# Router logits from the second norm's transposes: centred gate weights, context taken through the gates, choices for four tiles at a time

## What is computed

```
x = x + tanh(g_xattn[0]) * cross_attention_32_heads(layernorm(x), ctx)
x = x + tanh(g_ffn[0])   * (layernorm(x) @ W.T + bias)          # W dequantised
x = x + tanh(g_xattn[1]) * softmax(Q K.T * scale) @ ctx         # Q from layernorm(x), K from ctx
x = x + tanh(g_ffn[1])   * mixture_of_experts(layernorm(x))     # 32 experts, top 2
```

## Time and profile before

| what | us |
|---|---|
| median of 3 runs (883.96 to 884.87) | 884.09 |
| profiled execution | 882.28 |
| its span | 880.5 |
| first section (32 heads) ends | about 622 |
| first transposes of the second section (line 1803) | 622.53 |
| `score(0)` starts | 668.25 |
| `turn(0)` starts, the expert slots follow | 728.65 |
| TensorE's granted clock, mean over the span | 0.975 |

### The profile page before, as it was taken

One profiled execution on the slowest core, in us unless ns is written; L12 is line 12 of the kernel. 1 busy time (PEld: TensorE's weight loads), 2 busy tenths in 40 slices (PEclk: granted clock), 3 DMA queues, 4 the chain that ended last, 5 costly groups with the idle time before them and its releaser, 6 DMA issues. The chain is left out here.

```text
span 880.5 us, 13114 instructions
## 1 busy us (share of the span) xinstructions
PE 825.1 (94%) x4337; PEld 695.1 (79%) x4337; DVE 653.5 (74%) x1285; ACT 397.2 (45%) x1010; POOL 438.0 (50%) x386
## 2 busy tenths in 40 slices
PE   5889999999999999999999999999999999999980
PEld 4678888888888888888888888788778687778860
DVE  3888888867778876778876777856691658999965
ACT  4645245234334424324433433443314537879960
POOL 5489648436437634634833643530200148888840
PEclk9999999999999999999999999999999959999995
DMA  8401101101201100110220210100620677989517
GB/s 329 177 1 49 72 1 63 58 1 48 73 1 48 71 0 0 62 58 1 76 91 0 95 48 1 49 1 1 235 82 1 263 269 249 340 313 362 220 42 287
DMA packets 25945, 91.13 MB, mean 104 GB/s; under 512 B 6576, under 2 KB 7088, under 8 KB 18848
## 3 DMA queue, kind: packets, MB, share of 16 engines
q1 hardware_dynamic: 19744, 81.00, 25.1%
q0 software_dynamic: 6144, 9.46, 3.0%
HBM read 86.23 MB, written 14.68 MB: 115 GB/s over the span
## 5 line engine op out<-in xcount | busy, mean ns | idle before, releaser
L402 POOL TENSOR_TENSOR qT<-straight,turned 128x512 f32<-128x512 f32 x64 | 83.1, 1300 | 141.8 <-DVE turned L652 141.5
L518 ACT ACTIVATE probs<-bank,negmax 128x128 f32<-128x128 f32 x256 | 90.4, 365 | 130.8 <-DVE negmax L663 130.8
L652 DVE TENSOR_TENSOR turned<-bank,sinT 64x512 f32<-64x512 f32 x160 | 110.1, 688 | 2.2
L129 PE MATMUL bank<-xT_hi,wq_hi 128*128 128x512 f32 x256 | 104.2, 407 | 2.0 <-DVE xT_lo L105 2.0
L525 ACT ACTIVATE pT_hi<-bank 128x512 fp32r<-128x512 f32 x64 | 38.2, 598 | 139.0 <-PE bank L823 139.0
L131 PE MATMUL bank<-xT_hi,wq_lo 128*128 128x512 f32 x256 | 100.2, 392 | 0.0
L130 PE MATMUL bank<-xT_lo,wq_hi 128*128 128x512 f32 x256 | 100.0, 391 | 0.0
L131 PE MATMUL bank<-wo_hi,oT_lo 128*128 128x512 f32 x256 | 99.8, 390 | 0.0
L129 PE MATMUL bank<-wo_hi,oT_hi 128*128 128x512 f32 x256 | 99.7, 389 | 0.0
L130 PE MATMUL bank<-wo_lo,oT_hi 128*128 128x512 f32 x256 | 99.6, 389 | 0.0
L650 DVE TENSOR_TENSOR straight<-bank,cosT 128x512 f32<-128x512 f32 x80 | 55.3, 691 | 40.7 <-PE bank L131 36.9
(11 more groups left out here) (232 smaller groups left out, 2082.5 us busy)
## 6 DMA issues: line engine op xcount, KB each, us to landing
ring<-in_ew SPq DMA_DIRECT2D x28, 1024.0 KB, 8.8
raw_big<-in_wq SPq DMA_DIRECT2D x8, 1024.0 KB, 4.8
raw_big<-in_wo SPq DMA_DIRECT2D x8, 1024.0 KB, 4.8
early_w<-in_ew SPq DMA_DIRECT2D x8, 1024.0 KB, 10.0
ring<-picked SPq DMA_DIRECT2D x8, 512.0 KB, 7.6
raw_k<-in_wk SPq DMA_DIRECT2D x8, 256.0 KB, 5.1
ctx_raw<-in_ctxT SPq DMA_DIRECT2D x4, 512.0 KB, 6.1
raw_v<-in_wv SPq DMA_DIRECT2D x8, 256.0 KB, 5.0
```

The costliest lines, as they stand in the source:

```text
L129: nc.tensor.matmul(out_, hi, r_hi, start=start, stop=False)
L402: nc.gpsimd.tensor_tensor(dst, straight[:, k, :], turned[:, k, :], ALU.add).then_inc(rope_sum, 1)
L518: ex = nc.scalar.activation(probs[:, u % 2, h, :], bank_scores[u % 2][:, h * S:(h + 1) * S], ACT.Exp, bias=negmax[:, u % UNITS, h:h + 1], ...
L652: last = nc.vector.tensor_tensor(turned[dst, k, :], bank[src, :], sinT[src, tok], ALU.mult)
```

## The change

The last norm is linear in x up to a mean and a scale for each token, so a logit can be had without the normed row. The mean falls away if the gate weights are centred (from each column its mean is taken off). What is left is the centred gate on x, which is the second norm's turned tile times its own spread plus the attended part. The kernel after therefore makes, ahead of the router:

- on POOL, ACT and PE, the centred gate weights as an upper and a lower part side by side (`gate_pair`), with the mean from a matmul with a constant matrix;
- on PE, `wide(0..3)`: `gate_pair` times the context (0, 1) and times the turned second norm (2, 3), in 8 matmuls each; ACT keeps them (`wide_keep`), PE turns and joins the two parts (`wide_turn`);
- `ctx_gates` (ACT) and `base` (DVE) of these. The logits of four tiles are then one matmul each of the attention weights with `ctx_gates` (`gate_scores`), scaled and added to `base`.

`choose`, `code`, `find_place`, `rank` and the marks work on four tiles (marks on two) in place of one. The router's transposes, their copies on ACT and the old logits are gone. The order of SP's expert weights is changed, and ring slot 11 is no longer loaded at the section's start, since the new small tensors lie there. The diff, cut to its core:

```diff
@block.sync
-                for k in (*range(EARLY), RING):
+                for k in range(EARLY):
                     sp.dma_start(ring[k], a["ew"][k]).then_inc(w_in[k], 16)
...
+                sp.wait_ge(g_mm, 4 * KC)
+                first_weights(3, 4)
                 sp.wait_ge(g_smm, 2)
-                for k in (*range(EARLY, RING - 4), RING - 2, RING - 1):
-                    sp.dma_start(ring[k], a["ew"][k]).then_inc(w_in[k], 16)
-                keep_rows(TILES)
+                first_weights(2)
+                keep_rows(range(0, 4))
+                first_weights(5)
+                keep_rows(range(4, 6))
+                first_weights(6)
+                keep_rows(range(6, 8))
                 sp.wait_ge(g_omm, NB)
-                for k in range(RING - 4, RING - 2):
-                    sp.dma_start(ring[k], a["ew"][k]).then_inc(w_in[k], 16)
+                first_weights(7, 8, 9, 10)
+                sp.wait_ge(r_logits, 2)
+                first_weights(11)
@block.gpsimd
+                nc.gpsimd.memset(mean_of[:, :], 1.0 / E).then_inc(gate_step, 1)
+                pool.wait_ge(g_tables, 64)
+                pool.wait_ge(gate_step, 3)
+                nc.gpsimd.tensor_tensor(centred[:, :, :], gw[:, :, :], gate_mean[:, :].unsqueeze(1).broadcast_to([P, KC, NX]), ALU.subtract).then_inc(gate_step, 1)
+                pool.wait_ge(gate_step, 5)
+                nc.gpsimd.tensor_tensor(gate_pair[:, :, NX:], centred[:, :, :], gate_pair[:, :, 0:NX].bitcast(F32), ALU.subtract).then_inc(gate_step, 1)
                 weights_rest(1)
...
@block.scalar
                 for c in range(KC):
                     act.wait_ge(f_turned, c + 1)
                     nc.scalar.activation(wT_hi[:, c, :], psum[4 + c][:, :], ACT.Copy).then_inc(f_hi, 1)
+                act.wait_ge(gate_step, 2)
+                nc.scalar.activation(gate_mean[:, :], psum[2][:, 0:NX], ACT.Copy).then_inc(gate_step, 1)
                 norm_upper(act, 1, 4)
...
-                router_norm(0)
-                router_norm(1)
-                router_kept(0)
+                for t in range(0, 4):
+                    router_norm(t)
...
@block.vector
+                def choose(h):
+                    tiles = range(4 * h, 4 * h + 4)
+                    dve.wait_ge(gate_step, 8)
+                    dve.wait_ge(r_logits, h + 1)
+                    for b, t in enumerate(tiles):
+                        nc.vector.scalar_tensor_tensor(base[:, t, :], psum[1][:, t * NX:(t + 1) * NX], l1scale[:, b:b + 1], base[:, t, :],
+                                                       ALU.mult, ALU.add).then_inc(r_best, 1)
...
                 softmax_shift(0)
                 softmax_scale(0)
+                scale_base()
                 dve.wait_ge(g_tables, 64)
+                choose(0)
                 attended(0)
                 attended(1)
                 softmax_shift(1)
+                find_place(0)
                 attended(2)
                 attended(3)
                 softmax_scale(1)
+                mark_places(0)
+                mark_places(1)
+                choose(1)
+                normed(0)
                 attended(4)
-                normed(0)
                 attended(5)
+                find_place(1)
+                normed(1)
+                mark_places(2)
                 attended(6)
...
+                mark_places(3)
                 attended(7)
...
                 normed(2)
...
@block.tensor
+                def wide(n):
...
+                    for c in range(KC):
+                        if c:
+                            nc.tensor.matmul(bank[0:NX, :], gate_pair[:, c - 1, 0:NX], r_lo[:, c - 1, half_of(n % 2)], start=False, stop=False)
...
+                        mm = nc.tensor.matmul(bank[0:2 * NX, :], gate_pair[:, c, :], r_hi[:, c, half_of(n % 2)], start=c == 0, stop=c == KC - 1)
+                    mm.then_inc(wide_mm, 1)
+                def wide_turn(n):
+                    pe.wait_ge(wide_kept, 2 * n + 2)
+                    for t in TILES:
+                        mm = nc.tensor.matmul(psum[6 if n == 0 else 0][:, t * NX:(t + 1) * NX], wideT[:, t * P:(t + 1) * P], twin[:, :], start=True, stop=True)
+                    mm.then_inc(wide_turned, 1)
+                def gate_scores(n):
+                    pe.wait_ge(g_pkept, n + 1)
+                    pe.wait_ge(gate_step, 8)
+                    for b in range(4):
+                        t = 4 * n + b
+                        mm = nc.tensor.matmul(psum[1][:, t * NX:(t + 1) * NX], l1pT[:, b * S:(b + 1) * S], ctx_gates[:, t, :], start=True, stop=True)
                     mm.then_inc(r_logits, 1)
...
                     mm.then_inc(f_turned, 1)
+                pe.wait_ge(gate_step, 1)
+                pe.wait_ge(g_tables, 64)
+                for c in range(KC):
+                    mm = nc.tensor.matmul(psum[2][:, 0:NX], mean_of[:, :], gw[:, c, :], start=c == 0, stop=c == KC - 1)
+                mm.then_inc(gate_step, 1)
                 project(2 * KC - 1)
...
                 norm_turn(pe, 2, 1, last_xn)
+                wide(0)
                 forward(6)
...
                 project(11)
+                wide(1)
                 score(0)
                 project(12)
+                wide_turn(0)
                 project(13)
+                wide(2)
+                wide(3)
                 turn_probs(0)
                 project(14)
+                wide_turn(1)
+                gate_scores(0)
                 project(15)
                 attend(0, range(2))
                 score(1)
                 attend(0, range(2, 4))
+                rank(0)
+                turn_probs(1)
                 pe.wait_ge(constants, 2)
...
                 fill(0, 2)
...
+                gate_scores(1)
+                for t in range(2):
+                    codes(t)
+                attend(1, range(2))
+                for t in range(2, 4):
+                    codes(t)
+                rank(1)
+                attend(1, range(2, 4))
                 pe.wait_ge(g_added, NB)
...
+                for t in range(4, NB):
+                    codes(t)
                 fill(6, 16)
                 turn(0)
```

More of the change, by code:

```diff
@@ L1309, in _ @@
                 norm_sqrt(act, 3, HALVES[1])
+                for n in range(2):
+                    rows = slice(n * NX, (n + 1) * NX)
+                    nc.scalar.activation(twin[rows, :], ident[rows, rows], ACT.Copy)
                 for c in range(KC):
@@ L1317, in _ @@
                 norm_upper(act, 1, 7)
+                act.wait_ge(gate_step, 4)
+                nc.scalar.activation(gate_pair[:, :, 0:NX], centred[:, :, :], ACT.Copy).then_inc(gate_step, 1)
                 weights_upper(1)
                 norm_sqrt(act, 4, HALVES[0])
[L1320 to L1321 removed]
+                norm_upper(act, 2, 0)
+                norm_upper(act, 2, 1)
+                wide_keep(0)
+                norm_upper(act, 2, 2)
+                norm_upper(act, 2, 3)
                 keep(8)
@@ new lines, in choose @@
+                def choose(h):
[5 more added lines that the diff above has]
+                                                       ALU.mult, ALU.add).then_inc(r_best, 1)
+                    for b, t in enumerate(tiles):
+                        dve.wait_ge(r_best, 12 * h + b + 1)
+                        nc.vector.max(best[:, t, :], base[:, t, :]).then_inc(r_best, 1)
+                    for b, t in enumerate(tiles):
+                        dve.wait_ge(r_best, 12 * h + 4 + b + 1)
+                        nc.vector.max_index(best_at[:, t, :], best[:, t, :], base[:, t, :]).then_inc(r_best, 1)
+                    dve.wait_ge(r_best, 12 * h + 12)
+                    four = slice(4 * h, 4 * h + 4)
+                    nc.vector.tensor_tensor(onehot[:, four, :, :], numbers[:, 0:NX].unsqueeze(1).unsqueeze(1).broadcast_to([P, 4, TOP, NX]),
+                                            best_at[:, four, 0:TOP].unsqueeze(3).broadcast_to([P, 4, TOP, NX]), ALU.is_equal).then_inc(r_onehot, 1)
@@ new lines, in find_place @@
+                def find_place(h):
+                    four = slice(4 * h, 4 * h + 4)
+                    dve.wait_ge(r_rank, h + 1)
+                    nc.vector.tensor_tensor(weighted[:, :, :, :], onehot[:, four, :, :].bitcast(F32),
+                                            rank_bank(h)[:, 0:4 * NX].rearrange("p (t e) -> p t e", e=NX).unsqueeze(2).broadcast_to([P, 4, TOP, NX]),
+                                            ALU.mult).then_inc(r_place, 1)
+                    dve.wait_ge(r_place, 2 * h + 1)
+                    nc.vector.tensor_reduce(place[:, four, :], weighted[:, :, :, :], AX.X, ALU.add).then_inc(r_place, 1)
@@ L1714, in router_turn @@
                     for c in range(KC):
-                        mm = nc.tensor.transpose(router_bank(t)[:, c * P:(c + 1) * P], last_xn[:, t, c * P:(c + 1) * P], ident[:, :])
-                    mm.then_inc(r_turned, 1)
-                def logits(t):
-                    pe.wait_ge(g_tables, 64)
```

(17 more changed lines are left out.)

211 lines of the change are left out of this document (83 added, 128 removed).

## The result

The kernel after takes 909.02 us (median of 6 runs, 907.54 to 909.81), the kernel before 883.96 in the same comparison: 1.0285 times as long, 95% interval 1.0272 to 1.0298, or 25 us. The forecast was 905.8 in a range of 892 to 911. The profiled execution took 908.29 us with a span of 906.2 and a mean granted clock of 0.961.

The account below looks back on a forecast made before the run. PE and DVE were taken as near full, then PE, then a router ring of PE, ACT, DVE and POOL. Terms 12.8 + 1.7 + 1.85 + 2.0 + 2.1 + 1.3 = 21.7 on 884.1 gave 905.8, range 892 to 911.

Parts of the forecast that it names:

- The wait for the tables: Ahead of the means and project(7), PE stands until the last of four table loads lands at 637.0: 12.8 us.
- The rival without a wait: Tables already in by 624 at the second section's start, so PE does not wait: 889, chance 0.07.
- The clock behind it: After the wait PE runs 5.4 us at half clock: means 1.7, project(7) 1.85 longer.
- `wide(0)` and `wide(1)`: Context products ahead of score(0), 1.84 each, partly filling PE's idle time: 2.0 us added together.
- The router phase: From score(0) to turn(0): 62.5 against 60.4, so 2.1 us more, the norm coming last.
- the sum of 29.3 up to the end of `score(1)`: PE's work from score(0) to the end of score(1), including 0.7 of waiting for base: 29.3 us, before 20.5.
- DVE's list: From find_place(0) to attended(7), DVE's steps in written order set the pace, PE not being later: 18.5 us.
- The first slots: First expert slots, PE partly at half clock after standing between fill and turn(0): 1.3 us, up to 2.7.
- A phase that really shortens: Rival: DVE overlaps its steps, PE's queue limits the router phase, turn(0) at 49.7 after score(0): 891.8, chance 0.11.
- the forecast's 3.0 for a row in SP's queue: After the last norm, the row lands in DRAM in 3.0 us with one weight between rows.
- More lost: Rival: the clock falls ahead of codes, attends and ranks cost 2.5 more, slots 2.7, gather 8.3: 911, chance 0.13.
- The sums of 889 and 891.8 for two rivals: Totals if the tables cause no wait (889, chance 0.07) and if the router phase shortens (891.8, chance 0.11).

Follow-up runs that it names:

- experiment 1: Kernel before with one added PE wait for all four g_tables loads ahead of project(7), nothing else of the change; 900.59 us, ratio 1.0188.
- experiment 2: Kernel after with the gate means behind forward(3) on PE, and their ACT and POOL steps later too; 891.35 us, ratio 1.0112 to the kernel before.
- Experiment 7: Kernel after with gate_scores(0) behind project(15) and the first attends on PE, choose(0) behind attended(1) on DVE; 905.09 us, ratio 1.0258 to the kernel before.
- experiment 3: Kernel after with the gate weights' load on its own semaphore, so the means wait for gw alone; 903.06 us, ratio 1.0218 to the kernel before.
- experiment 4: Kernel after with 38 unused 512-column matmuls on PE ahead of the wait for the tables; 907.03 us, ratio 1.0286 to the kernel before.
- experiment 5: Kernel after with expert weights 7 to 11 held on SP until slots 0 and 1's tokens are turned; 905.92 us, ratio 1.0259 to the kernel before.
- experiment 12: experiment 11 with choose(1) earlier and find_place(0) later on DVE, rank(1) and four tiles' codes earlier on PE; 881.52 us, ratio 0.9995 to the kernel before.
- experiment 11: Kernel after: means late, router lists reordered, weights 7-11 held, gate_scores(0) later, weights 5 and 6 ahead of rows, six early gathers; 882.64 us, ratio 0.9996.

## Why the prediction was right, and where its sizes were off

**The wait for the tables: right.** 12.8 forecast, 12.75 in the profile, and by itself 16.6 of 25 us with the clock behind it (experiment 1). The rival without a wait is out.

**The clock behind it: right, slightly short.** Means 1.70 as forecast; `project(7)` 2.18 longer, forecast 1.85, since the clock rose 6.5 us after work began and not 5.4. The lower clock also slowed the transposes ahead of the wait, which cost nothing under it.

**`wide(0)` and `wide(1)`: right.** What is left of the 18.53 beside 12.75, 1.70 and 2.18 is 1.90, forecast 2.0; 1.9 also in experiment 2.

**The router phase: right in kind, half its size.** `gate_scores(0)` stood 20.8 after `score(0)` (forecast 20.5), and the norm was last. The step that was mis-sized is the sum of 29.3 up to the end of `score(1)`: it took 31.5, since it priced the 0.7 of waiting for `base` but not the clock that falls there. `project(15)` paid 1.42 for it; the other 0.8 is spread over the terms. Experiment 7 takes the wait and the low clock away, and 29.0 comes out, against 28.6 for the same sum without its 0.7. Behind that the terms were 22.6 to the last norm (forecast 23.2), 4.5 from there to POOL's gather (forecast 3.0: the row took 3.65, and 0.8 went by until POOL issued), and 6.0 to `turn(0)` (forecast 7.0).

**DVE's list: the number right by luck.** DVE ran from `find_place(0)` at 721.94 to the last attended tile at 740.1 in 18.2 (forecast 18.5) with no gap over 0.9. But the forecast held that PE is not the later one there, and in this profile it was. The chain that ended last runs on PE at the lower clock from 727.10 to 736.23, and DVE's largest gap, 0.89, is a wait for `rank(1)`:

```profile
734.32 1.91 PE bank L1744 x2
736.25 0.76 DVE x L1461
```

In experiments 3, 4, 5 and 7 the clock was up again ahead of these attends (1.96 for four in place of 3.41), and the same stretch of DVE took 16.7 to 17.1. So the list alone was priced about 1.5 too high, and PE's lower clock filled in 1.2 of that. Little of the 1.2 would have reached `turn(0)`: in those four runs the last row took 4.4 to 5.4 to land.

**The first slots: the number right by luck.** The total is 1.42, forecast 1.3 for the lower clock alone. From `turn(0)` to the third slot's transposes it took 8.19 (752.93 to 761.12) in place of 4.88: 3.3 lost, of which 1.16 is a wait for the second gather and the rest the clock, 0.50 in 756 to 758. The later slots do not give this back, and none of them waits for a load of expert weights. What gives back 1.9 lies behind the last slot, where the chain goes through POOL's last write of results (before, then after):

```profile
856.14 3.79 DMA picked<-summed,place_row
883.78 2.07 DMA picked<-summed,place_row
```

It lands in 2.1 in all twelve traces with the change, and in 3.8 and 3.7 in the two without (the kernel before and experiment 1). The forecast took all that follows the first slots to be the same in both kernels; why the write lands sooner is open.

**Not in the sum:** 1.50 in the first section, which the diff doesn't touch. In 22 to 44 us the clock was 0.92 where before it was 1.00. The start of the second section lay between 622.50 and 624.69 over all runs here, both ends in kernels with the change, so this belongs to the execution; why the clock fell there is open. It and the 2.15 of the phase are nearly all of the 4.0 by which the difference of the profiled spans (25.7) exceeds the forecast's 21.7.

**The rivals.** A phase that really shortens was there to be had, and the order of two queues kept it away: repaired, it is 57.2, and 55.2 in experiment 12. The forecast's 3.0 for a row in SP's queue was near only because the norms were late; with earlier norms the rows behind the weights took 7.9 to 9.1. It was also measured by a load of 64 KB, where a row is 256 KB. More lost came in part: the clock did fall ahead of the codes, but most of PE's slower work was hidden behind DVE's list, and the gather took 6.0 and not 8.3. The sums of 889 and 891.8 for two rivals leave out the 1.3 of the first slots without a reason.

**The whole.** Out of the 25.1 us, 15.3 come back by moving the means, and the rest by the orders of PE's, DVE's and SP's lists. What remains is nearly even: by the profile of experiment 11, 2.8 more ahead of `score(0)` against 3.2 less up to `turn(0)` and 1.4 less behind it, with 0.7 more in the first section. No version tried is faster than before by more than the measurement can tell.

## What to carry to other kernels

A new use of a tensor inherits the wait of its semaphore: here one `wait_ge` counted four loads for the sake of one, and cost 17 us at the head of an engine's list (experiment 1); look up when the last of the counted loads lands, and place the use behind that. A DMA that something waits for should not stand behind megabytes in its queue that nobody needs yet, and this shows only once the work ahead of it gets faster. When a change is split into its parts, the parts that were slow only for their place come back whole, and what is left is the worth of the idea: here nothing that can be measured.

## What the runs showed that was not expected

- Before the granted clock went to 0.50 at about 710, PE had done eight matmuls of 32 columns (16 records, 1.97 us), stood 0.68 us and begun four more, with no longer idle time of PE near; with `gate_scores(0)` moved away, it stayed at 1.00.
- A row of 256 KB took 2.0 us to land with no weight in flight ahead of it. With weights between the rows the last row took 3.65 to 5.4 with late norms, and 7.86 and 9.05 with norms that came 5.9 and 9.5 us sooner.
- With the slots' weights sent later, DMA runs at 403 to 413 GB/s in 736 to 766 us (experiments 11 and 12), where before it was 314 to 344, and PE showed a wait for a gather only when slots started 2 us sooner still.
